# Loading the sampling positions of a deformable convolution with four long transfers per batch in place of twelve short ones

## What is computed

```python
om = conv3x3(x, w_off) + b_off                      # 27 maps per image
off_y, off_x, mask = om[:, :9], om[:, 9:18], sigmoid(om[:, 18:])
py = off_y + h + ky                                 # where each of 9 taps samples
px = off_x + w + kx
sampled = bilinear(x, py, px) * mask                # zero outside the image
out = einsum('bckhw,ock->bohw', sampled, w) + b
out = relu(batchnorm(out) * gamma + beta) + x
```

## Time and profile before

| quantity | value |
|---|---|
| median of 3 runs | 2031.7 us (2031.66 to 2035.28) |
| profiled execution, its own time | 2033.44 us |
| span of the profiled execution | 2031.6 us |
| DVE busy over the span | 1557.3 us (77%) |
| PE busy over the span | 1417.8 us (70%) |
| ACT busy over the span | 1205.9 us (59%) |
| DMA packets, bytes | 278516, 464.92 MB |

### The profile page before, as it was taken

One profiled execution on the slowest core, in us unless ns is written; L12 is line 12 of the kernel. 1 busy time (PEld: TensorE's weight loads), 2 busy tenths in 40 slices (PEclk: granted clock), 3 DMA queues, 4 the chain that ended last, 5 costly groups with the idle time before them and its releaser, 6 DMA issues. The chain is left out here.

```text
span 2031.6 us, 59696 instructions
## 1 busy us (share of the span) xinstructions
PE 1417.8 (70%) x24174; PEld 947.6 (47%) x24175; DVE 1557.3 (77%) x1719; ACT 1205.9 (59%) x1755; POOL 394.4 (19%) x753
## 2 busy tenths in 40 slices
PE   3775994000008998999999999999999998985510
PEld 3652331000005666666666666666666666664210
DVE  5354001998738999999999999999999999995216
ACT  1221224565206787787787788787787787774102
POOL 2000003665210211212212112111211212122000
PEclk9787997555558999999999999999999999998655
DMA  9056886899999999999998999999999999990009
GB/s 257 3 150 170 238 246 165 271 355 300 308 259 255 246 258 242 254 258 246 251 253 250 253 252 253 257 244 252 259 248 253 256 240 259 242 233 24 4 1 389
DMA packets 278516, 464.92 MB, mean 229 GB/s; under 512 B 71520, under 2 KB 235223, under 8 KB 274665
## 3 DMA queue, kind: packets, MB, share of 16 engines
q1 hardware_dynamic: 252276, 425.39, 76.6%
q0 software_dynamic: 20944, 21.53, 4.0%
q10 hardware_dynamic: 5030, 14.25, 2.2%
HBM read 354.01 MB, written 106.93 MB: 227 GB/s over the span
## 5 line engine op out<-in xcount | busy, mean ns | idle before, releaser
L1018 PE MATMUL ps_even_v<-tent_x,stage 32*128 32x171 f32 (+3 forms) x5568 | 533.7, 319 | 114.1 <-DVE G L1140 112.9
L1094 ACT COPY even_v<-ps_even_v 128x1008 f32<-128x1008 f32 (+2 forms) x464 | 450.4, 971 | 261.9 <-PE ps_odd_v L1018 261.9
L1140 DVE TENSOR_TENSOR G<-odd_y,ps_odd_v 128x1008 f32<-128x1008 f32 (+1 forms) x448 | 533.9, 1192 | 48.8 <-PE ps_odd_v L1018 34.8
L1018 PEld LDWEIGHTS ps_even_v<-tent_x,stage 32*128 32x128 f32 x5568 | 431.8, 186 | 264.7 <-issue 264.3
L1148 DVE TENSOR_TENSOR G<-even_v,ps_even_y 128x1008 f32<-128x1008 f32 (+2 forms) x464 | 538.5, 1161 | 1.7
L1018 PE MATMUL ps_odd_v<-tent_x,stage 32*128 32x171 f32 (+3 forms) x5568 | 534.9, 321 | 0.4 <-issue 0.4
L1037 PE MATMUL ps_r<-G,conv_w 128*32 128x224 f32 (+3 forms) x9264 | 479.1, 333 | 4.0 <-issue 3.1
L1018 PEld LDWEIGHTS ps_odd_v<-tent_x,stage 32*128 32x128 f32 x5568 | 422.7, 186 | 0.0
L1001 PE MATMUL ps_odd_y<-rows,sel 32*128 32x504 f32 (+1 forms) x448 | 218.7, 488 | 274.2 <-DMA rows<-scratch_parts 272.9
L949 POOL DMA_DIRECT2D scratch_conv<-res x448 | 215.4, 487 | 932.6 <-ACT res L1101 897.5
L1037 PEld LDWEIGHTS ps_r<-G,conv_w 128*32 128x32 f32 x9264 | 263.9, 109 | 165.3 <-issue 112.9
(11 more groups left out here) (170 smaller groups left out, 1044.3 us busy)
## 6 DMA issues: line engine op xcount, KB each, us to landing
place<-scratch_px SPq DMA_DIRECT2D x768, 147.0 KB, 3.5
odd_y<-scratch_full SPq DMA_DIRECT2D x576, 196.0 KB, 4.9
rows<-scratch_parts SPq DMA_DIRECT2D x192, 220.5 KB, 4.9
x<-scratch_xh SPq DMA_DIRECT2D x48, 406.0 KB, 6.1
stage<-scratch_xt SPq DMA_DIRECT2D x192, 96.0 KB, 4.4
scratch_parts<-parts SPq DMA_DIRECT2D x6, 2688.0 KB, 12.8
scratch_om<-om ACTq DMA_DIRECT2D x64, 196.0 KB, 7.2
scratch_full<-tent_y SPq DMA_DIRECT2D x12, 784.0 KB, 9.2
```

Source lines behind the costliest of these rows:

```text
L1018: m = nc.tensor.matmul(sub(ps_v[g % 2], 0, 128, i * 512 + lo + first, dims), stage[32 * g:32 * g + 32, j * IMAGE + v * C:j * IMAGE + (v + ...
L1094: nc.scalar.copy(two(even_v[(STEPS * it + p) % 2], ROW, 2 * p), two(ps_v[0], 512, 2 * p)).then_inc(even_kept, 1)
L1140: nc.vector.tensor_tensor(sub(G, 0, 128, slot(it, v) + lo, [[ROW, 2]] + straight), weights, sub(ps_v[1], 0, 128, lo, [[512, 2]] + straight ...
```

## The change

`load_place` issues one transfer for each group of 32 partitions, with a run of 14112 bytes per partition, in place of three with 4704 bytes each. The order of the groups, the bytes, the source rows and the place in SP's program stay. The count of transfers that readers wait for follows.

```diff
-            PER_PLACE, PER_ROWS, PER_WIDE = 12, 3, KK
+            PER_PLACE, PER_ROWS, PER_WIDE = 4, 3, KK
...
                 def load_place(pair, n):
-                    for ky in range(3):
-                        for g in (0, 2, 1, 3):
-                            sp.dma_start(sub(place[n % 2], 32 * g, 32, ky * PIECE, [[1, PIECE]]),
-                                         dram("px", ((n * B + pair * 2) * 2 + g) * BATCH + ky * PIECE, [[0, 32], [1, PIECE]])
-                                         ).then_inc(place_loaded[n % 2], 16)
+                    for g in (0, 2, 1, 3):
+                        sp.dma_start(sub(place[n % 2], 32 * g, 32, 0, [[1, BATCH]]),
+                                     dram("px", ((n * B + pair * 2) * 2 + g) * BATCH, [[0, 32], [1, BATCH]])
+                                     ).then_inc(place_loaded[n % 2], 16)
```

## The result

The changed kernel takes 2244.3 us (2240.1 to 2246.0, four runs), the kernel before 2033.5 in the same comparison: a ratio of 1.1024 with a 95% interval of 1.0999 to 1.1049. The profiled execution of the changed kernel took 2240.1 us with a span of 2238.3, which is 206.7 us more than the span of before. The forecast was 2032.2 us, the range ended at 2038, and even the slower rival stopped at 2070.

What follows compares the result with a forecast made beforehand. The prediction took DVE's own instructions to bound the loop. Only the start counted, +0.5 us for a slower first `place` batch; SP and loop terms were 0. Span 2031.6 became 2032.1 us, median 2032.2 us, range 2028 to 2038.

Steps and rivals of the forecast that it cites:

- the slower rival: In the loop, DMA engines become the bound and DVE waits for wide weights in every batch: +38 us, 2070 us; chance 0.14.
- That no data would be late: In the loop, slower `place` batches fit into 1.8 us of free engine time; no wait is added, value 0.
- That the loop is bound by DVE: In the sampling loop, DVE's own instructions set the pace; in steady state no transfer is waited for.
- The rate of long runs: DMA engines move the 14112-byte runs of `place` at 230 GB/s, with 225 and 283 as ends.
- The start of the block: First `place` batch takes 7.85 us, not 7.3, delaying the first product into `G`: +0.5 us, bounds -0.9 and +0.7.
- The rule of the Trainium skill that the prediction weighed: 32 SBUF partitions are reached through 8 of 16 ports, limit about 218 GB/s; the start would lose 1.0 us.
- the one on SP: SP makes 8 issues fewer per batch, freeing about 4 us in the loop, worth nothing: value 0, bounds -3.7 and 0.
- The first rival: The same as the slower rival: in the loop, transfers sum to 19.9 us per batch, above 19.2; 2070 us, chance 0.14.
- Second rival: At the block's start SP sets the pace, so eight issues fewer give back 3.7 us: 2028.0 us; chance 0.10.
- Third rival: The 14112-byte runs of `place` go out as several packets, so everything stays as it is, 2031.7 us; chance 0.06.

Runs made afterwards that it cites:

- experiment 5: The changed kernel, with SP in the loop waiting for ACT's next step between the four long `place` transfers, one per step: 2062.6 us, ratio 1.0155.

## Why the prediction was wrong, point by point

**That no data would be late** held: DVE's only wait for a transfer is the one at the start. **That the loop is bound by DVE** held for the kernel before and not for the changed one: DVE's busy time is unchanged, but it waits 242.1 us for PE.

**The rate of long runs** was sized nearly right: 230 GB/s taken, 225 to 238 as the nearest rows, 221 measured in the loop. In the stretch from 589 to 594, while the first batch moves, it is 225; over the whole window of the earlier trace rows, 587 to 595, it is 200 with a share of 0.97, under the forecast of 225 to 240:

```profile
589.00:594.00 5.00, 0.00 (x0) 0.00 (x0) 0.00 (x0) 0.00 (x0) 0.00 (x0) 0.50 1.07 225
587.00:595.00 8.00, 0.00 (x0) 0.00 (x0) 1.29 (x1) 0.00 (x0) 0.55 (x2) 0.50 0.97 200
```

The start of the block moved a little more than the bounds of the term, +0.5 with 0.7 as its end: the first product into `G` begins at 607.25 in both traces, but in the changed kernel SP had started its issues at 584.83 and not at 585.89, so it comes 1.1 us later after them. The rule of the Trainium skill that the prediction weighed, on the page "SBUF — State Buffer", section "Door 1: The DMA port swizzle", with about 218 GB/s and 1.0 us, came nearest on both.

**The step that failed** is the one on SP: "In the loop it is worth nothing: nobody waits for SP or for what it issues". It priced eight issues less as saved time of SP, worth between -3.7 us and 0. The freed 4.8 us per batch are a change of pace, from 1.81 MB in 6.5 us, about the engines' own rate, to 1.81 MB in 1.7 us. The term was not mis-sized but had the wrong sign: it cost about 180 us, as experiment 5 gives back with SP's pace alone, by spreading the same four issues over 8 us. A sign of it stood in the earlier trace rows: while twelve issues of `place` went out the engines' share was 0.92, below that of full engines, which suggests that SP held them back. The prediction counted only data among what moves on the DMA engines and left out PE's instruction blocks, though the page lists their queue (q8).

**The first rival** had the side but not the mechanism. It expected the sum of the transfers' times to pass 19.2 us per batch and DVE to wait for `odd_y`. The DMA share fell instead, to 0.88. **Second rival:** nothing was won at the start. **Third rival:** the packets did change, though by 24580, not by the 16384 of the prediction: the changed kernel has 8192 long packets in place of 24576 short ones, and another 8192 packets under 512 bytes are gone, 128 for each of the 64 batches, 16 for each transfer dropped.

What stays open: how an engine chooses between its queues. The records of packets don't name the engine, so it is not seen directly that a block stands behind `place` on the same one. What is shown is that 45 of the 55 gaps end 2.4 to 3.1 us after a block starts, and that the waits rise and fall with SP's pace and with the time that other queued transfers take to land. How much of the 31 us in experiment 5 is rate and how much queue was not separated.

## What to carry to other kernels

An unrolled program is itself a stream of data that moves by DMA beside the tiles, about one 16 KB block every 7 us of PE's work here; before many issues are joined into few, ask how many bytes will then stand in the queue at once, not only how many bytes move. The number of issues can act as a throttle that nobody wrote down: if it is removed, replace it by a wait on progress. In a profile the sign is an engine idle under "issue" in the middle of a row of like instructions, with the granted clock falling in it or behind it.

## What the runs showed of the hardware that was not expected

- With more data queued, instruction blocks started too late for PE: 45 stops of 2.2 us on average (100.3 us), up to 4.3 us. A stop may bring a stretch at half the granted clock (1.00 to 0.50 between 1108.3 and 1108.4 us, back by 1116; 36 stretches in the loop). PE's busy time grew by 83.6 us, its "issue" waits by 121.5 us.
- With the same bytes and runs, the order of transfers over groups of 32 partitions (0, 2, 1, 3 against three of each in a row) moved the median landing from 3.5 to 4.5 us and the kernel by 2.0% (1.2% to 2.8%).
- Runs of 4704 or 14112 bytes made no difference beyond 16 us of 2230 when transfer size and pace were the same.
- Eight issues of 16 strided partitions took SP 5.5 us (median over the loop), eight of 32 partitions 3.65 us, though the bytes were equal and the page counts 8192 packets fewer (258034 against 266226). No run here explains it.
